# The final weighted sum of a two-layer decoder: how the expert outputs are grouped for their loads, and which engine adds which of them

## The reference

```python
logits = jnp.einsum('th,eh->te', x, gate_w)
probs = jax.nn.softmax(logits, axis=-1)
topk_w, topk_idx = jax.lax.top_k(probs, TOP_K)                 # 8 of 64
combine = (one_hot(topk_idx, NUM_EXPERTS) * topk_w[..., None]).sum(axis=1)
for each expert e:
    h = silu(x @ w13_e[:INTER].T) * (x @ w13_e[INTER:].T)
    out = out + combine[:, e, None] * (h @ w2_e.T)
x = layernorm(x + out)                                         # 1024 x 256
```

## Time and profile before

| | |
|---|---|
| median of three runs | 794.01 us |
| the profiled execution | 784.39 us, of which the span in the trace is 783.1 us |
| TensorE, VectorE, ScalarE, GpSimd busy | 713.5, 510.0, 342.8, 300.8 us |
| mean granted clock of TensorE | 0.979 of 2.4 GHz |
| all 18 loads of the final sum (L2091) | 10 of 512 KB, 8 of 384 KB |
| first of them issued, last one landed | 747.5 us, 775.4 us |
| last output written by ScalarE | 781.4 us |

### The profile page before, as it was taken

How to read it: one execution, slowest core, us unless ns; L and a number is a source line. 1 busy time by engine, 2 the same in 40 slices (tenths; PEclk the granted TensorE clock), 3 DMA queues, 4 the chain that set the end, 5 groups by cost and what they waited for, 6 DMA issues and landing times.

```text
span 783.1 us, 16549 instructions
## 1 busy us (share of the span) xinstructions
PE 713.5 (91%) x5435; PEld 586.8 (75%) x5444; DVE 510.0 (65%) x1673; ACT 342.8 (44%) x906; POOL 300.8 (38%) x395
## 2 busy tenths in 40 slices
PE   6999999998899999999998788772899999999986
PEld 4667778786778888888887445441799999999965
DVE  4888777775466666666767778752456666655535
ACT  4454556442344344444433245551344444466525
POOL 1112121322115212121213006777666666666545
PEclk9999999999999999999999999995899999999999
DMA  9444080000024233263321346863698999944367
GB/s 228 106 128 128 17 287 15 8 1 1 20 75 149 75 98 126 76 165 88 109 68 35 122 112 177 263 248 107 217 350 240 322 312 326 350 140 122 112 228 276
DMA packets 83607, 118.03 MB, mean 151 GB/s; under 512 B 28087, under 2 KB 58397, under 8 KB 83268
## 3 DMA queue, kind: packets, MB, share of 16 engines
q1 hardware_dynamic: 74356, 99.63, 41.8%
q0 software_dynamic: 9168, 17.35, 6.1%
HBM read 102.36 MB, written 35.58 MB: 176 GB/s over the span
## 4 chain that ended last, share of the span: by engine, by line
PE 76%; POOL 6%; DVE 5%; issue 4%; DMA 4%; ACT 3%; SPq 2%; DVEq 0%; ACTq 0%; POOLq 0%
PE ps L187 69%; PE ps L190 7%; POOL x_slots L1650 3%; DVE topc L1552 2%; ACT pTc L1497 1%; DMA rowso<-y_slots 1%; DMA x<-in_x_in 1%; DMA y_slots<-o_e,index_e 1%; SPq L334 1%; POOL y_slots L2019 1%; DMA rows_e<-x_slots 0%; DMA x_slots<-rows_all,index_all 0%; SPq L2091 0%; ACT eT L555 0%; POOL kkc L1618 0%
## 5 line engine op out<-in xcount | busy, mean ns | idle before, releaser
L2019 POOL DMA_INDIRECT y_slots<-o_e,index_e x127 | 124.4, 979 | 72.3 <-issue 60.5
L187 PE MATMUL ps<-xT_e,w_slot 128*128 128x128 f32 x760 | 101.3, 277 | 0.0
L187 PEld LDWEIGHTS ps<-xT_e,w_slot 128*128 128x128 f32 x760 | 93.4, 194 | 0.0
L1998 DVE TENSOR_TENSOR h_e<-ps,gate_e 128x128 f32<-128x128 f32 x127 | 37.0, 291 | 76.6 <-ACT gate_e L1959 76.4
L1650 POOL DMA_INDIRECT x_slots<-rows_all,index_all x64 | 62.7, 979 | 19.7 <-issue 18.1
L1953 ACT COPY xT_e<-ps 128x256 f32<-128x256 f32 x127 | 47.3, 373 | 45.6 <-PE ps L190 41.6
L187 PE MATMUL ps<-x_hi,w_hi 128*128 128x512 f32 x192 | 62.2, 405 | 3.1 <-DVE x_lo L1059 1.5
L1959 ACT ACTIVATE gate_e<-ps 128x128 f32<-128x128 f32 x127 | 35.3, 278 | 67.5 <-PE ps L187 67.5
L187 PE MATMUL ps<-x_lo,w_hi 128*128 128x512 f32 x192 | 59.6, 391 | 0.0
L187 PE MATMUL ps<-x_hi,w_lo 128*128 128x512 f32 x192 | 59.3, 390 | 0.0
L1139 POOL TENSOR_TENSOR w_lo<-wh,w_hi 128x256 fp32r<-128x256 f32 x48 | 34.0, 735 | 63.4 <-ACT w_hi L1002 63.4
(11 more groups left out here) (301 smaller groups left out, 1709.4 us busy)
## 6 DMA issues: line engine op xcount, KB each, us to landing
w_slot<-in_we SPq DMA_DIRECT2D x95, 384.0 KB
rows_e<-x_slots SPq DMA_DIRECT2D x127, 136.0 KB
x_slots<-blank SPq DMA_DIRECT2D x4, 2176.0 KB, 10.1
sums<-key_sums SPq DMA_DIRECT2D x15, 512.0 KB, 4.4
w_kept<-in_we SPq DMA_DIRECT2D x20, 384.0 KB, 4.7
wh<-in_wqkv SPq DMA_DIRECT2D x16, 384.0 KB, 5.5
rowso<-y_slots SPq DMA_DIRECT2D x10, 512.0 KB, 6.8
w_early<-in_we SPq DMA_DIRECT2D x12, 384.0 KB, 5.1
```

Source lines behind the costliest of these rows:

```text
L187: return self.pe.matmul(out, lhsT, rhs, start=start, stop=stop, skip_group_check=shared)
L1998: dve.tensor_tensor(T.h[:, :], T.g_bank[:, P:2 * P], T.gate[:, :], ALU.mult).then_inc(*t.h.one)
L2019: pool.indirect_dma_start(m.y_slots, bass.IndirectOffsetOnAxis(ap=T.index[:, :], axis=0), T.o[:, :], None, bounds_check=TOK * TOPK - 1, oo ...
```

## The change

Places 1 and 2 become two groups, each with two loads of four sequences (512 KB as before); place 1 waits for all scatters but the last six, place 2 for all but five. ScalarE and GpSimd take place 3 instead of place 5; TensorE takes place 5 and no longer place 3, so that it has places 5, 6 and 7 of every sequence. On GpSimd `root` b - 2, not `root` b - 1, follows `add` b. `LAST_LOADS` names the same loads by the new numbers. The table of places, filled on GpSimd in the second layer's attention, needs one IOTA per group: five instead of four.

```diff
-GROUPS = ((0, 1), (1, 3), (3, 5), (5, 8))
+GROUPS = ((0, 1), (1, 2), (2, 3), (3, 5), (5, 8))
...
-BY_POOL = 5
+BY_POOL = 3
...
-LAST_LOADS = ((2, 0), (2, 1), (3, 0), (3, 1), (2, 2), (3, 2), (3, 3), (2, 3), (3, 4), (3, 5), (3, 6), (3, 7))
+LAST_LOADS = ((3, 0), (3, 1), (4, 0), (4, 1), (3, 2), (4, 2), (4, 3), (3, 3), (4, 4), (4, 5), (4, 6), (4, 7))
...
-        self.rows_in = [over[0:2], over[2:6], over[6:10], [ev.dma(f"sum_in{b}", 1) for b in range(NSEQ)]]
+        self.rows_in = [over[0:2], over[2:4], over[4:6], over[6:10], [ev.dma(f"sum_in{b}", 1) for b in range(NSEQ)]]
...
-    for g in range(2):
+    for g in range(len(GROUPS) - 2):
         landed(g)
         for part in range(len(t.rows_in[g])):
             load(g, part)
...
     add_group(1, range(NSEQ))
+    add_group(2, range(NSEQ))
     for g, part in LAST_LOADS:
...
     for b in range(NSEQ):
         add(b)
-        if b:
-            root(b - 1)
+        if b >= 2:
+            root(b - 2)
+    root(NSEQ - 2)
     root(NSEQ - 1)
```

## The result

The change makes the kernel slower: ratio of the times 1.0056, 95% interval 1.0033 to 1.0079 (22 runs each). In us that is 4.4 (2.6 to 6.2). The medians, 794.32 us after and 790.86 us before, differ by 3.5 us. Ratios leave out runs more than 1.5% above the fastest run of the same kernel. A later set of ten runs gave 1.0028 (0.9992 to 1.0064), which can't be told from no change.

The account below looks back on a forecast made before the run. Late loads bounded the last stretch; after the change, a closed chain of queues. Loads 2.1 us earlier, then five turns of 2.73 us, ended the span at 785.9, 2.8 us later; added to the 794.01 median: 796.8 us, range 794.8 to 799.5.

Parts of the forecast that it names:

- Place 1's loads at 748.8: SP's load issue: place 1 waits for an earlier scatter, so its loads go out at about 748.8, not 753.14.
- rival (a): Loads behind group 0: they come no earlier, the end is 5.2 us late, 799.2 us; chance 0.14.
- The gain of 2.1 us for the first load of the last group: DMA loads: closing the rate hole gains 2.46 us, smaller rows cost 0.37; first landing at 763.75, not 765.85.
- The 1.53 us from that landing to sum 0: TensorE: three products, run-out and two handovers lead to VectorE's sum of sequence 0, 1.53 us after the landing, at 765.28.
- Root 0 after 1.37 us, beside an addition of VectorE: GpSimd: root 0 comes 1.37 us after VectorE's sum 0, at 766.65; VectorE's addition beside it costs 0.17 us once.
- Five turns of 2.73 us: GpSimd: roots 1 to 5 each wait one turn of root, output, weighing and addition; 2.73 us each, 13.65 in all.
- 3.67 and 1.72 us to the end: ScalarE: from root 5 through the last outputs takes 3.67 us, then 1.72 us to the end of the span.
- The tables of places, costed at nothing: GpSimd at 253 us: one IOTA more, 0.19 us at most, costed at nothing beside weight preparation that waits for ScalarE.
- Rival (b), TensorE at 1.2 GHz: TensorE before the last group: low clock makes sequence 0's three products take 2.6, not 1.3 us; 798.1 us; chance 0.09.
- Rival (c), faster: Last group: the closed chain doesn't set the pace, TensorE sets the end at 780.3; 791.2 us; chance 0.07.
- the ring: Closed chain across GpSimd and ScalarE: root, output, weighing, addition, next root; one turn of 2.73 us per sequence.
- The shorter turn, 2.2 to 2.45 us: Closed chain: a turn below its bound, 2.2 to 2.45 us, ending up to 1.6 us late; chance 0.09.

Follow-up runs that it names:

- the kernel before on the slower set: The kernel before, unchanged, profiled a second time in a set where it ran at about 865 us; tail 28.09 us.
- the order of the roots alone: The kernel before with only GpSimd's new order, root b-2 behind addition b; ratio 1.0092 to the kernel before, tail 35.31 us.
- the kernel with the old roots: The changed kernel with GpSimd's old order put back, root b-1 behind addition b; ratio 0.9969 to the kernel before, tail 27.80 us.

## Why the prediction was right

The forecast was slower by 2.8 us, 796.8 us, with 794.8 to 799.5 us about it. It was drawn up from the kernel before at 794.01 us. Timed side by side, the kernel before stood at 790.86, so it is the change that is to be compared and not the 794.32 us: 794.01 x 1.0056 is 798.5 us. Measured: slower, by 4.4 us in the times (2.6 to 6.2), 3.4 us in the tails of the two profiles and 2.3 us in the later pair.

The mechanism was the right one, and the part that the trace could give came out closely: from sum 0 to the end the forecast has 20.6 us, and the two profiles have 20.9 and 20.7. That the mean of the two pairs of tails, 2.85 us, falls on the forecast is luck in part: the gain in the loads was about 1 us too large for the kernel in general (below), and against the second profile of the kernel before the cost of the chain was 0.8 us too large, since that one took 16.5 us from sum 0 to the end and not 15.7. Point by point, against the tail forecast for the changed kernel, 785.86 - 754.22 = 31.64 us; it was 32.26:

- **Place 1's loads at 748.8.** They went out at -5.56 from the last scatter, 748.66 on the clock of before. Place 2's at -1.25, 752.97 for 753.14. The scatter's lag (1.31 us in the forecast, 1.18 here) and the queueing behind group 0 were read rightly, and rival (a) didn't happen.
- **The gain of 2.1 us for the first load of the last group.** 1.95 us in this pair of profiles. Over all profiles it is less: with five groups the load landed at 9.22 us in the mean of nine, with four at 10.31 in the mean of four. The hole is not always 2.75 us wide. In the kernel before on the slower set, SP issued the load of place 1 and 2 at -5.20 and not at -1.08, since there two of the last scatters come 3.6 us apart. The term was right for the trace it was read from and, with 1.1 us between the two means, about 1 us too large for the kernel in general.
- **The 1.53 us from that landing to sum 0.** 1.72 us; TensorE began 0.15 us after the landing, not 0.03.
- **Root 0 after 1.37 us, beside an addition of VectorE.** 1.37; its shift came 0.84 us later, the forecast had 0.81. The forecast did not ask what addition 2 ahead of root 0 needs; the 1.37 us held because place 3 made weighing 2 early, as the order of the roots alone showed. The Trainium skill, "SBUF — State Buffer", section on its two separate sides, states that a VectorE instruction with two SBUF inputs and a GpSimd instruction that reads SBUF exclude one another. The trace agrees: VectorE's addition of sequence 3 runs from 771.65 to 772.12, over the start of the root at 771.81, and the root takes 0.74 us there and 0.55 alone.
- **Five turns of 2.73 us.** 14.01 us from root 0 to root 5, 13.82 forecast. The rest is root 3, which met another addition of VectorE (0.73 us).
- **3.67 and 1.72 us to the end.** 3.68 and 1.80.
- **The tables of places, costed at nothing.** They cost 0.12 us ahead of the tail; the cover of the weight preparation was not there.
- **Rival (b), TensorE at 1.2 GHz.** Around the first landings of the last group TensorE was busy for 1.87 of 3.00 us, and the granted clock stayed at 2.4 GHz (1.00), as it did in the stretches shown further above. So the rival's price stays untried:

```profile
765.00:768.00 3.00, 1.87 (x7) 1.10 (x8) 1.36 (x3) 1.11 (x3) 0.95 (x2) 1.00 1.01 383
```

- **Rival (c), faster.** It is the kernel with the old roots, and there the mechanism of (c) was wrong in size: 1.1 us less tail than before, not 2.8. Sum 7 came 6.1 us after the landing of sequence 4's load, where I had 5.4 by TensorE: it waited for addition 7 and this for weighing 7, which stands behind output 4 in ScalarE's queue. Also the slow stretch put that load at 16.98 and not at 16.0. So in that kernel TensorE alone is not the next limit. ScalarE's own work is close behind its 1.29 us per sequence: outputs start 1.45 us apart in the kernel before where ScalarE has no idle time (770.13 and 771.58). In all nine profiles without the ring the end comes 7.1 to 8.5 us after the last landing.
- **The shorter turn, 2.2 to 2.45 us.** It didn't happen: no turn was shorter than 2.72 us.

What the times add to the tails (4.4 for 3.4 us) lies within the interval of the ratio. If the 1.1 us of the clock at 504 to 580 us is the change's, it belongs here too, with the 0.12 us of the IOTA; the runs don't settle it.

Of the versions tried, the five groups with place 5 and the old order of the roots is the best candidate: both of its ratios are under 1 and its tails, 26.70 and 27.69 us, are under both of the kernel before. That it is faster is not shown, as said above of its first ratio.

## What to carry to other kernels

When an instruction is moved behind another in one engine's queue, follow what that other waits for, through each queue in turn, until the path ends or comes back. If it comes back to the moved instruction of an earlier round, its handovers add up to a price per round that no busy time shows, and the slack that the waits of the old order show says nothing about it. And a gain in loads is worth only what it takes off the last landing: measure from a fixed event shortly before, since spans of the same kernel differ by more than the gain.

## What was not expected of the hardware

The DMA engines, with loads queued the whole time, fell below the 390 to 410 GB/s of the stretches beside, for 2 to 4 us. In seven of the thirteen profiles that was plain 9 to 12 us behind the last scatter (271 GB/s after, 324 with five groups), in the first of the kernel before at 3 to 5 us (293 GB/s); in these stretches some of SP's issues took 1.0 us instead of 0.45. From the first to the last landing of the last group it takes 10.6 to 11.5 us in those seven profiles and 9.5 to 10.2 in the other six, so it costs about a microsecond of the last landing. It stayed unexplained. The last landings of one kernel differ by 1.0 and 2.4 us between two executions (last load of before 21.17 and 20.20, of the changed kernel 20.65 and 18.22), more than most edits of the loads are worth.
